# Who issues the q stacks, and when: sliding-window attention with a channel mix on one core

## The reference

```python
q = (x @ Wq + bq)   # 16 heads of 16, in 4 groups
k, v = x @ Wk + bk, x @ Wv + bv   # 4 groups of 16
scores = einsum('bghqd,bgkd->bghqk', q, k) / 4
# a query i sees the keys i-127 to i
out = softmax(scores) @ v
x = layernorm(x + out @ Wo + bo)
x_prev = x shifted by one token
xr, xk = mu_r * x + (1 - mu_r) * x_prev, mu_k * x + (1 - mu_k) * x_prev
x = layernorm(x + sigmoid(xr @ W_r.T) * (square(relu(xk @ W_k.T)) @ W_v.T))
```

## Time and profile before

| | |
|---|---|
| Time, median of 3 runs | 492.97 us (490.83 to 494.72) |
| The profiled execution | 496.05 us |
| Its span, first to last instruction | 494.0 us |
| TensorE busy (matmuls) | 408.5 us, 83% |
| VectorE busy | 340.5 us, 69% |
| GpSimd busy | 287.1 us, 58% |
| ScalarE busy | 272.9 us, 55% |
| Mean granted TensorE clock | 0.913 of full |
| DMA | 39.24 MB, mean 79 GB/s |

### The profile page before, as it was taken

One profiled execution on the slowest core, in us unless ns is written; L12 is line 12 of the kernel. 1 busy time (PEld: TensorE's weight loads), 2 busy tenths in 40 slices (PEclk: granted clock), 3 DMA queues, 4 the chain that ended last, 5 costly groups with the idle time before them and its releaser, 6 DMA issues.

```text
span 494.0 us, 8282 instructions
## 1 busy us (share of the span) xinstructions
PE 408.5 (83%) x2494; PEld 252.1 (51%) x2494; DVE 340.5 (69%) x851; ACT 272.9 (55%) x566; POOL 287.1 (58%) x466
## 2 busy tenths in 40 slices
PE   5407686998799978998799888998699979999964
PEld 2104344565455645665455554665455646765542
DVE  5506653588677886688677875688677987996541
ACT  3301343665656764776477563776466566877521
POOL 5500343575747775676567684676557785787521
PEclk9857687999999998999899996999999998999965
DMA  7780583035902393146704391146703390000000
GB/s 297 138 100 7 115 168 49 10 81 88 182 12 58 77 189 47 37 107 108 129 13 89 77 187 17 38 106 105 131 13 70 86 118 12 23 14 23 12 21 21
DMA packets 50124, 39.24 MB, mean 79 GB/s; under 512 B 32929, under 2 KB 41633, under 8 KB 49953
## 3 DMA queue, kind: packets, MB, share of 16 engines
q1 hardware_dynamic: 43024, 25.74, 23.2%
q10 hardware_dynamic: 7056, 12.98, 16.9%
HBM read 26.38 MB, written 12.06 MB: 78 GB/s over the span
## 4 chain that ended last, share of the span: by engine, by line
PE 47%; DMA 24%; ACT 8%; DVE 6%; POOL 4%; issue 4%; ACTq 4%; SPq 1%; POOLq 0%; DVEq 0%
DMA qs<-q_parts 22%; PE proj_ps L876 8%; PE av_ps L963 7%; PE score_ps L949 6%; PE gen L997 5%; PE max_ps L932 4%; PE gen L1054 4%; ACTq L512 4%; PE gen L1043 4%; PE gen L1032 3%; ACT probs L521 3%; POOL probs L386 2%; PE max_ps L923 2%; DVE q_tiles L680 2%; ACT parts L492 2%
## 5 line engine op out<-in xcount | busy, mean ns | idle before, releaser
L386 POOL TENSOR_SCALAR_AFFINE_SELECT probs<-probs 128x512 f32<-128x512 f32 x252 | 165.8, 668 | 121.2 <-ACT probs L521 118.1
L521 ACT ACTIVATE probs<-score_ps 128x512 f32<-128x512 f32 x252 | 148.4, 598 | 112.1 <-PE score_ps L949 94.6
L949 PE MATMUL score_ps<-qs,ks 98*128 98x512 bf16 x252 | 100.8, 403 | 15.7 <-ACT probs L521 12.7
L688 DVE TENSOR_REDUCE neg_max<-max_ps 128x3 f32<-128x480 f32 x144 | 87.3, 631 | 18.9 <-PE max_ps L932 18.2
L963 PE MATMUL av_ps<-probs,vals 128*32 128x512 f32 x504 | 67.9, 613 | 0.9 <-POOL probs L386 0.8
L949 PEld LDWEIGHTS score_ps<-qs,ks 98*128 98x128 bf16 x252 | 25.0, 100 | 73.3 <-ACT probs L521 58.4
L393 POOL TENSOR_TENSOR rstd<-var,minus_half 128x1 f32<-128x1 f32 x64 | 35.7, 558 | 34.3 <-DVE var L712 33.7
L876 PE MATMUL proj_ps<-x_t,first 128*128 128x512 f32 x88 | 47.0, 660 | 10.0 <-DMA first<-w_first 5.4
L932 PE MATMUL max_ps<-ks,q_tiles 96*128 96x160 bf16 x416 | 53.3, 247 | 0.0
L1043 PE MATMUL gen<-mix,rest_w 128*128 128x128 f32 x256 | 38.5, 298 | 13.1 <-DVE mix L763 11.9
L680 DVE COPY q_tiles<-qs 96x2048 bf16<-96x2048 bf16 x32 | 25.8, 810 | 33.9 <-DMA qs<-q_parts 33.9
(11 more groups left out here) (74 smaller groups left out, 636.1 us busy)
## 6 DMA issues: line engine op xcount, KB each, us to landing
qs<-q_parts ACTq DMA_DIRECT2D x48, 256.0 KB, 11.1
q_parts<-parts SPq DMA_DIRECT2D x48, 128.0 KB, 2.2
x_t<-x_feat SPq DMA_DIRECT2D x8, 512.0 KB, 9.3
x_in<-x_nat SPq DMA_DIRECT2D x8, 512.0 KB, 12.5
out<-out_t SPq DMA_DIRECT2D x32, 128.0 KB, 2.0
ks<-k_parts SPq DMA_DIRECT2D x42, 80.0 KB, 3.0
k_parts<-parts SPq DMA_DIRECT2D x8, 192.0 KB, 2.8
rest_w<-w_rest SPq DMA_DIRECT2D x1, 1152.0 KB, 7.7
```

What stands on the lines that cost most here:

```text
L386: nc.gpsimd.affine_select(out=v, in_=v, compare_op=ALU.is_ge if i % 2 else ALU.is_gt, fill=0.0, base=0, pattern=[[0, HPG], [sign, BLK]], c ...
L521: nc.scalar.activation(probs[:, buf, i], score_ps[i % 2][:, :], ACT.Exp, scale=SCALE).then_inc(s_exp, 1)
L688: nc.vector.tensor_reduce(neg_max[:, TPB * i:TPB * i + n], max_bank(t, j, i)[:, 0:n * TILE_KEYS].rearrange("p (n k) -> p n k", k=TILE_KEYS ...
L949: nc.tensor.matmul(score_ps[i % 2][:, :].rearrange("p (h q) -> p h q", q=BLK), ks[0:ROWS + MPARTS, par, g, k0:k0 + BLK], qs[0:ROWS + MPART ...
```

## The change

On every superblock: `stack_q` moves from ScalarE to SyncE, in step j = 1 behind the rows, where `load_x` was; `load_x` moves to step j = 2, behind that step's rows. At the start: the three chunks of the second superblock are projected into the banks `gen0`, `gen1` and `av_ps`, ahead of the maxima; ScalarE stacks only block 0 of q (six transfers of 64 KB), which with the k stacks has a semaphore of its own, `s_stack0`; SyncE stacks the other three blocks (six transfers of 192 KB) once these have landed, ahead of block 0's rows; the tile copy of block 1 comes after the maxima of block 0; GpSimd's low parts stand ahead of and between its two sums with bo.

```diff
 SyncE
-                    sp.dma_start(ks[rep * DH:(rep + 1) * DH, par, :, WINDOW:], src[:, :, 0:SB]).then_inc(s_stack, 16)
+                    sp.dma_start(ks[rep * DH:(rep + 1) * DH, par, :, WINDOW:], src[:, :, 0:SB]).then_inc(s_stack0, 16)
+            def stack_q(s, par, rep):
+                if rep == 0:
+                    sp.wait_ge(s_spill_q, s * SPILLS + SPILLS)
+                    if later(s, 2):
+                        sp.wait_ge(s_score, scored(s * SB_BLKS - SB_BLKS - 1, NSCORE - 1))
+                sp.dma_start(qs[rep * DH:(rep + 1) * DH, par].rearrange("d j (m x) g t -> d (j m) (x g t)", m=QCH),
+                             q_dram[par, Q_PART[rep]].rearrange("j m (d y) t -> d (j m) (y t)", d=DH)
+                             ).then_inc(s_stack, 16)
 start:
                 for rep in range(NREP):
                     stack_k(0, 0, rep)
+                sp.wait_ge(s_stack0, STACKS)
+                for rep in range(NREP):
+                    sp.dma_start(qs[rep * DH:(rep + 1) * DH, 0, 1:].rearrange("d j (m x) g t -> d (j m) (x g t)", m=QCH),
+                                 q_dram[0, Q_PART[rep], 1:].rearrange("j m (d y) t -> d (j m) (y t)", d=DH)
+                                 ).then_inc(s_stack, 16)
                 max_in(0, 0, 0)
 step:
-                if coming and j == 1:
+                if project and j == 1:
+                    for rep in range(NREP):
+                        stack_q(s + 1, 1 - par, rep)
+                if coming and j == 2:
                     load_x(s + 2, par)
 GpSimd, start
-                x_plus_bo(0, 0)
                 for m in range(NCH):
                     low_part(0, m)
+                x_plus_bo(0, 0)
+                low_part(1, 0)
                 x_plus_bo(1, 1)
-                for m in range(NCH):
-                    low_part(1, m)
+                low_part(1, 1)
+                low_part(1, 2)
 ScalarE, start
-                high_part(1, 0)
+                high_part(1, 0, gen0)
+                high_part(1, 1, gen1)
+                middle_part(1, 0)
+                high_part(1, 2, av_ps)
+                act.wait_ge(s_spill_q, SPILLS)
                 for rep in range(NREP):
-                    stack_q(0, 0, rep)
-                middle_part(1, 0)
-                high_part(1, 1)
+                    act.dma_start(qs[rep * DH:(rep + 1) * DH, 0, 0].rearrange("d (m x) g t -> d m (x g t)", m=QCH),
+                                  q_dram[0, Q_PART[rep], 0].rearrange("m (d y) t -> d m (y t)", d=DH)
+                                  ).then_inc(s_stack0, 16)
                 middle_part(1, 1)
-                high_part(1, 2)
                 middle_part(1, 2)
 ScalarE, step
-                if project and j == 1:
-                    for rep in range(NREP):
-                        stack_q(s + 1, 1 - par, rep)
 VectorE
-                if j == 0:
-                    dve.wait_ge(s_stack, s * STACKS + STACKS)
+                if s == 0 and j == 0:
+                    dve.wait_ge(s_stack0, STACKS)
+                elif j == (1 if s == 0 else 0):
+                    dve.wait_ge(s_stack, s * STACKS + STACKS // 2)
 start:
-                rest_part(1, 0)
-                rest_part(1, 1)
+                rest_part(1, 0, gen0)
+                rest_part(1, 1, gen1)
+                rest_part(1, 2, av_ps)
+                val_copy(1, 1)
                 tile_q(0, 0, 0, 0)
-                tile_q(1, 0, 1, 0)
                 for i in range(NMAXB):
                     tile_max(0, 0, i)
                 turn_max(0, 0)
-                rest_part(1, 2)
-                val_copy(1, 1)
+                tile_q(1, 0, 1, 0)
 TensorE
 project_chunk:
-                    if later(s, 1):
+                    if later(s, 2):
                         pe.wait_ge(s_val, s)
 v_turn:
-                pe.wait_ge(s_rest, s * NCH + (NCH if later(s, 1) else 1))
+                if s == 1:
+                    pe.wait_ge(s_val, 1)
+                else:
+                    pe.wait_ge(s_rest, s * NCH + (NCH if later(s, 1) else 1))
 start:
-                for m in range(QCH):
-                    project_chunk(1, m, 1)
+                for m in range(NCH):
+                    project_chunk(1, m, 1, (gen0, gen1, av_ps)[m])
+                v_turn(1)
                 pe.wait_ge(s_zero, 5)
                 pe.wait_ge(s_masks, 2 + TPB)
                 for i in range(NMAXB):
                     max_scores(0, 0, 0, i)
-                    if i == 1:
-                        project_chunk(1, QCH, 1)
-                v_turn(1)
```

More of the change, by code:

```diff
@@ L177, in attention_channel_mix @@
         s_stack = sem("s_stack")
+        s_stack0 = sem("s_stack0")
         s_tiles = sem("s_tiles")
@@ L503, in middle_part @@
                 nc.scalar.copy(parts[:, m, 1], rest[:, m]).then_inc(s_mid, 1)
[L505 to L514, removed]
             def exps(t, i, buf):
```

## The result

The changed kernel takes 464.61 us (median of 4 runs, 462.40 to 467.47), the kernel before in the same runs 492.33. The ratio is 0.9436, with a 95% interval of 0.9368 to 0.9504. The profiled execution took 467.47 us, its span is 465.7.

The account below looks back on a forecast made before the run. No engine is full; waits bound the kernel, chiefly TensorE's idle time around the late q stack and the start. 12.7 + 13.8 + 0.8 + 2 = 29.3 us off 496.05 gives 466.8, said as 466, range 461 to 471 (70%).

Parts of the forecast that it names:

- 12.7 us: Superblock 0: TensorE restarts behind the stack of superblock 1 at 68.2 instead of 80.91, 12.7 us earlier.
- 13.8: Ordinary superblocks 1 to 5: step 3 restarts 2.75 us earlier in each, 13.8 us in all.
- Step 0 at 39.4: Start: step 0 begins at 39.4 instead of 47.60, 8.2 us earlier, after the three-block stack and half a tile copy.
- The step on the rows of block 1: Superblock 0: TensorE's 2.16 us wait for these rows goes, as SyncE is free of k stacks before they are ready.
- the terms of -0.9 and 2.2: Superblock 0: 0.9 us charged for step 0 restarting at 1.2 GHz; 2.2 us gained from the vanished rows wait.
- +16.55: Ordinary superblock: step 3's restart, counted from SyncE's issue of the j = 1 rows; stack lands +15.8, then tile copy.
- Removed: six issues on ScalarE, so TensorE's 1.53 us: Ordinary superblock: without ScalarE's six stack issues, TensorE's 1.53 us idle time before score 7 goes.
- +19.36 - 1.12 - 1.53 = +16.7: Ordinary superblock: TensorE's own arrival at step 3, the old restart less 1.12 us stack wait and 1.53 us issue wait.
- The +18.2 of superblock 2: Kernel before: TensorE's arrival at step 3 with its ScalarE stall, counted from SyncE's issue of the j = 1 rows.
- The rival on TensorE at 2.4 GHz: Ordinary superblocks: TensorE at full rate arrives near +15; an early stack gives up to 1.5 us more each, 459; 7%.
- The sign I had named against myself: Listed as showing the prediction wrong: stretches at 1.2 GHz in most superblocks.
- The clock term: Long low-clock stretches: less idle time ahead of them spares 2 us, range 0 to 5.8.

Follow-up runs that it names:

- x_late_only: The kernel before with only the x loads moved from step j = 1 to j = 2, ScalarE still issuing the stacks; 470.70 us, ratio 0.9569.
- steps_only: The kernel before with only the change in the steps (stacks on SyncE behind the rows, x loads one step later), old start; 473.20 us, ratio 0.9610.
- start_x_late: The changed kernel with the q stacks issued by ScalarE again in the steps, new start and later x loads kept; 459.76 us, ratio 0.9276.
- two_queues: Against start_x_late, the six stack copies shared: ScalarE issues 0 to 2, SyncE 3 to 5 behind its rows; 457.42 us, ratio 0.9224.

## Why the prediction was right, and where it was not

**Total and place.** 466 was said and 464.6 measured. Superblock 0 was to bring 12.7 us and brought 13.0 by the restart, 13.7 by the rows of j = 1 in superblock 1 (117.51 to 103.82). The five ordinary superblocks were to bring 13.8 and 2 for the clock.

Worked out from the traces, from the rows of j = 1 at 103.82 to those at 364.99 the changed kernel takes 261.2 us; before it took 392.42 - 117.51 = 274.9. That is 13.7 us, clock included, for 15.8. Superblock 6 was to bring 0.8 and its two stretches are 0.9 shorter (12.67 + 11.72 against 13.55 + 11.71). So 1 us too little for superblock 0 and 2.1 too much for the ordinary ones with their clock partly cancel; that part of the agreement is luck.

**The start.** Step 0 at 39.4 was said, 38.22 came. The first stacks landed at 26.2, 1 us sooner: their issue began at 21.39 for 21.9, beside ScalarE's bank reads, and each landed in 2.5 to 3.0 us for 3.1. The other three blocks landed in 11.3 us, as said (26.22 to 37.5). The step on the rows of block 1 is undecided: the 2.16 us wait was to vanish with SyncE's queueing. In the profiled execution 1.91 remained, and in the other profile of the same kernel it was gone, so SyncE's queueing alone does not set it. In the profiled one, only 0.6 us were gained from step 0 to that score (8.8 for 9.4) where the terms of -0.9 and 2.2 said 1.3, and the sooner step 0 made up for it: the rows of block 2 left at 51.35, for 51.7.

**The ordinary superblock.** Right: the stack's landing from first issue, 14.5 us (156.0 to 158.5 + 12.0), about +15.7 for +15.8; x_t lands in 4.4 us (median) and nobody waits for it. Near: restart at +16.2 to +17.3 for +16.55. TensorE waits 0.39 us for the stack in superblock 1 and 0.25 at most in the four others, where it runs at 1.2 GHz for a while behind the mixes and comes that much later itself. Wrong: the step "Removed: six issues on ScalarE, so TensorE's 1.53 us" and TensorE's arrival at "+19.36 - 1.12 - 1.53 = +16.7". x_late_only arrives at +16.5 with those 1.53 us still there. The +18.2 of superblock 2 had 1.7 us of 1.2 GHz in it; I read one superblock with a lowered clock as the pace, took the issue wait off it and got the right place with the wrong part; that was luck. Superblock 2 did not stand for all five: superblocks 1 and 5 of before have TensorE waiting 2.45 and 2.90 us for the stack, ready at +16.7 and +16.6. The rival on TensorE at 2.4 GHz had read the low clock in the same rows, but took the 1.53 us off as well, to +15; in the two profiles of the changed kernel it is ready at +15.8 at the earliest in superblocks 1 to 5. What the runs put in the step's place: the x loads give everything the steps give. The move to SyncE gives nothing or a small loss, because 0.6 us of longer wait for the mixes, a stack 0.8 us later and more low clock eat it.

**The sign I had named against myself** did come up: stretches at 1.2 GHz in four of five superblocks of this profile, two of five in the other profile of the same kernel. The clock term was as uncertain as its range, not as small as its value.

## What to carry to other kernels

Of two transfers that share the DMA engines, order them by who is waited for first; here one line that moved a load behind an urgent stack did as much as all the edits to the steps. Read TensorE's own pace from a stretch at full clock, or the price of a wait is taken from work that was only slow. Read a short wait in a second profile of the same kernel before explaining it: one of 1.91 us here was gone in the next. And shortening a wait ahead of a fixed landing gained nothing here until the landing moved: the same edit gained nothing alone and was in the kernel that is 5% faster once the transfer was issued earlier.

## What the runs showed of the hardware

The clock was lowered more often behind one idle time of 2.6 us than behind two of 1.5 and 2.0 us with work between them. Of the second stretches of superblocks 1 to 5, six of ten in two profiles of the changed kernel had a granted clock below 1.00, and one of ten in x_late_only and start_x_late. This is a tendency: steps_only, with the 2.6 us, has it in two of five, and two_queues, with 2.0 us and one of about 0.5, in two of five as well. A VectorE copy of 16 columns took 2.1 to 2.3 us beside GpSimd's 2.36 us sum, and 0.5 to 0.7 where the sum was cut into blocks of 0.7 us. Six 256 KB copies into 16 partitions each take 13.5 to 15.7 us from first issue on one queue and 13.2 to 14.8 on two, and 17.5 to 18.5 with 1 MB of x loads on another queue beside them. On one queue with them, 512 KB of x issued ahead landed in 3.5 us, and issued behind in 11.6 to 14.8.
